# A branch hint at the top of every iteration of the expert loops and of the weight-tile loop

## What is computed

```
scores = softmax(xf @ gate_w.T);  topv, topi = top_k(scores, 2)
h  = relu(einsum('ecd,ehd->ech', de, fc1_w) + fc1_b)     # de: tokens sorted by expert
eo = einsum('ech,ehd->ecd', h, fc2_w) + fc2_b
out = x + sum(gathered eo * gates)
```

## Time and profile before

| | us |
|---|---|
| median of 3 runs | 1538.37 (1534.41 to 1542.68) |
| span of the profiled execution, first to last instruction | 1528.3 |
| TensorE matmuls busy | 1458.1 (95%) |
| VectorE busy | 820.2 (54%) |
| ScalarE busy | 537.3 (35%) |
| GpSimd busy | 285.5 (19%) |

### The profile page before, as it was taken

How to read it: one execution, slowest core, us unless ns; L and a number is a source line. 1 busy time by engine, 2 the same in 40 slices (tenths; PEclk the granted TensorE clock), 3 DMA queues, 4 the chain that set the end, 5 groups by cost and what they waited for, 6 DMA issues and landing times.

```text
span 1528.3 us, 21024 instructions
## 1 busy us (share of the span) xinstructions
PE 1458.1 (95%) x6470; PEld 1196.0 (78%) x6470; DVE 820.2 (54%) x1484; ACT 537.3 (35%) x871; POOL 285.5 (19%) x342
## 2 busy tenths in 40 slices
PE   7569999999999999999999999999999999999996
PEld 5348888788887888788887888788887888888885
DVE  6756634575355824566345753568245662558311
ACT  4234422343233422344233432344223432344221
POOL 1040030301204031120303121130312103030301
PEclk9669999999999999999999999999999999999998
DMA  8456431774319732394318742296324943196100
GB/s 291 179 138 146 100 102 36 160 146 106 75 41 180 151 97 55 96 175 98 110 28 160 159 103 65 53 190 134 91 55 107 174 90 103 34 181 137 56 0 27
DMA packets 446304, 169.30 MB, mean 111 GB/s; under 512 B 405248, under 2 KB 407433, under 8 KB 444274
## 3 DMA queue, kind: packets, MB, share of 16 engines
q1 hardware_dynamic: 293218, 84.01, 25.7%
q0 software_dynamic: 18096, 52.35, 12.1%
q10 hardware_dynamic: 134880, 31.47, 10.1%
HBM read 127.00 MB, written 41.03 MB: 110 GB/s over the span
## 4 chain that ended last, share of the span: by engine, by line
PE 95%; DVE 2%; issue 1%; DMA 0%; POOL 0%; ACT 0%; SPq 0%; DVEq 0%; POOLq 0%
PE hp L831 15%; PE hp L830 15%; PE eo L843 15%; PE eo L842 15%; PE eo L847 15%; PE hp L832 15%; PE hp L855 1%; PE eo L805 1%; PE hp L787 1%; PE hp L788 1%; DVE y_half L713 0%; DVE x_turned L713 0%; DMA rows<-in_x,gather_row 0%; PE xp L794 0%; DVE yT_lo L698 0%
## 5 line engine op out<-in xcount | busy, mean ns | idle before, releaser
L669 DVE TENSOR_TENSOR h_lo<-h_full,h_hi 128x512 fp32r<-128x512 f32 x256 | 176.6, 690 | 537.7 <-ACT h_full L451 537.6
L831 PE MATMUL hp<-yT_lo,w1T_hi 128*128 128x512 f32 x1020 | 397.7, 390 | 16.3 <-issue 16.3
L830 PE MATMUL hp<-yT_hi,w1T_hi 128*128 128x512 f32 x1020 | 398.1, 390 | 0.4 <-issue 0.2
L842 PE MATMUL eo<-w_hi,h_hi 128*128 128x512 f32 x1024 | 398.3, 389 | 0.0
L843 PE MATMUL eo<-w_lo,h_hi 128*128 128x512 f32 x1024 | 398.3, 389 | 0.0
L832 PE MATMUL hp<-yT_hi,w1T_lo 128*128 128x512 f32 x1020 | 397.5, 390 | 0.0
L448 ACT ACTIVATE h_hi<-hp,b_now 128x512 fp32r<-128x512 f32 x256 | 176.1, 688 | 617.7 <-PE hp L832 613.0
L847 PE MATMUL eo<-w_hi,h_lo 128*128 128x512 f32 x1024 | 273.7, 389 | 0.0
L832 PEld LDWEIGHTS hp<-yT_hi,w1T_lo 128*128 128x128 f32 x1020 | 192.0, 188 | 57.3 <-issue 17.6
L830 PEld LDWEIGHTS hp<-yT_hi,w1T_hi 128*128 128x128 f32 x1020 | 191.8, 188 | 42.1 <-issue 2.4
L842 PEld LDWEIGHTS eo<-w_hi,h_hi 128*128 128x128 f32 x1024 | 192.3, 188 | 40.0
(11 more groups left out here) (146 smaller groups left out, 717.0 us busy)
## 6 DMA issues: line engine op xcount, KB each, us to landing
w_raw<-in_L_ffn_fc_w SPq DMA_DIRECT2D x512, 64.0 KB
w_raw<-in_L_ffn_fc_w SPq DMA_DIRECT2D x128, 256.0 KB, 3.1
slots_dram<-x_blk ACTq DMA_DIRECT2D x30, 512.0 KB, 3.6
x_blk<-slots_dram ACTq DMA_DIRECT2D x240, 64.0 KB
out<-x_all SPq DMA_DIRECT2D x8, 1024.0 KB, 12.3
x_all<-in_x SPq DMA_DIRECT2D x7, 1024.0 KB, 13.9
b_bc<-in_L_ffn_fc_b POOLq DMA_DIRECT2D x8, 256.0 KB
x_all<-in_x SPq DMA_DIRECT2D x4, 256.0 KB, 4.1
```

What stands on the lines that cost most here:

```text
L669: dve.tensor_tensor(h_lo[:, c, :], h_full[:, :], h_hi[:, c, :].bitcast(F32), ALU.subtract).then_inc(h_ready, 1)
L830: pe.matmul(bank, w1T_hi[:, hh, q, :], yT_hi[:, par, q, :], start=(q == 0), stop=False)
L831: pe.matmul(bank, w1T_hi[:, hh, q, :], yT_lo[:, par, q, :], start=False, stop=False)
L842: pe.matmul(eo[:, b, :], h_hi[:, c, blk], w2_hi[:, hh, :], start=(hh == 0), stop=False)
```

## The change

The two loop heads are written with the general form of the same loop, for the same engine and the same range, with `hint_back_edge=True`. With it, each iteration begins with one more instruction on that engine, a branch prefetch hint, which names the compare-and-branch that closes the loop as likely taken. Nothing else is added or moved. The helper `experts` is used by four engines, so five loops get the hint. The last expert, written out, has none.

```diff
         def experts(eng, body):
 
-            with eng.Fori(0, E - 1) as e:
+            with nc.Fori(0, E - 1, engines=[eng.engine], hint_back_edge=True) as e:
                 body(e, False)
             body(E - 1, True)
...
-            with sp.Fori(1, E * HT // RAW) as m:
+            with nc.Fori(1, E * HT // RAW, engines=[sp.engine], hint_back_edge=True) as m:
                 for c in range(RAW):
                     sp.wait_ge(w1_T, RAW * m + (c - RAW + 1))
```

## The result

| | kernel before | changed kernel |
|---|---|---|
| median of the timed runs, us | 1536.39 (1531.74 to 1542.68, 4 runs) | 1510.38 (1509.55 to 1510.87, 4 runs) |
| span of the profiled execution, us | 1528.3 | 1507.9 |
| first to seventh closing branch of TensorE, us | 1065.0 | 1044.5 |

The ratio is 0.9834, with a 95% interval of 0.9801 to 0.9867: 26.0 us or 1.7% faster. Forecast were 1521 us and a range of 1515 to 1540. The direction and the place were right; the size was not, since the measured time lies 4.6 us under the range, and what the hint does there was not what the prediction took it to do.

The account below looks back on a forecast made before the run. TensorE was taken to set the time, losing 20.5 us at six loop back edges. The terms, -20.5 + 0.6 + 2.5 + 0.3 = -17.1 us, took 1538.4 to 1521.3, predicted 1521 us, range 1515 to 1540.

Parts of the forecast that it names:

- The base: Whole kernel: the median's 10.1 us above the profiled span stays unchanged, so the gain is subtracted from 1538.4 us.
- The 20.5 us at the edges: TensorE's six loop back edges: time lost beyond six whole bodies of 174.08 us, 20.5 us, counted as gain.
- The costs set against them: Remaining losses with the hint: 0.6 for TensorE's second fetch, 2.5 for VectorE, 0.3 for the last iteration.
- second fetch partly bare: Behind each TensorE back edge: the unhinted fetch of the next code block may start late; 0.1 us each, 0.6 in all.
- tile 2 late by VectorE: TensorE waits after each edge for a tile VectorE prepares, if VectorE's hint fails: 5.0 us, half taken, 2.5.
- last iteration falls through: Loop end: the hint says taken but the branch falls through, at worst one more TensorE fetch; 0.3 us taken.
- hint instructions: One more instruction per iteration on each hinted engine, including SyncE's 63: hidden, 0 us.
- What happens in one edge: TensorE's back edge: two code fetches in a row, the first hidden by the full queue, the second bare; 3.5 us lost.
- What the hint does: TensorE's back edge: the target's block comes in before the branch, so the second fetch moves under the full queue, 0.4 us spare.
- R1: TensorE's loop: the prefetched target may be thrown out before the branch, so all stays, 1538 us; chance 0.15.
- R2: TensorE's body: the armed hint displaces ordinary prefetch, so blocks are fetched on demand; slower, 1558 us; chance 0.10.
- R3: TensorE's edges: target prefetched but second fetch not covered, 1.5 to 2.5 us of 3.4 stay; 1527 to 1533; chance 0.10.

Follow-up runs that it names:

- the head at slot 200: Kernel before, no hint, with TensorE's loop head alone placed at instruction place 200 of a 256-instruction code block: 1515.05 us, ratio 0.989.
- TensorE at slot 0: Kernel before, no hint, with the loop heads of TensorE and VectorE placed at the first instruction of a code block: 1509.77 us, ratio 0.9855.
- the late hint at slot 239: Changed kernel with TensorE's hint some 33 instructions ahead of the branch and its loop head held 17 places ahead of a code block's end: 1522.54 us.
- the late hint: Changed kernel with TensorE's hint moved to some 33 instructions ahead of the closing branch, loop head not held in place: 1509.97 us, ratio 0.9856.

## Why the prediction was wrong in size

**The base: the step that failed most.** "The median of the runs lies 10.1 us above this span, which I take as unchanged." In the changed kernel the median lies 2.5 us above the profiled span. That is 7.6 of the 10.9 us by which 1521.3 missed; the other 3.3 are the costs below. Even with all costs at zero this base gave 1517.9. Outside the span there are only 1.6 to 2.1 us, in 29 later runs of the kernel before and the four of the changed one. So the rest of the 10.1 were longer spans of the other executions; and where a second and a third profile show such a span (1532.9 and 1535.9), the added time lies at the edges, most of it in the slower clock after more of the pauses. These are the pauses that the change removes, so this part of the spread goes with them: the changed kernel's four runs lie within 1.3 us, those of before within 11. Of the 26.0 us gained, 20.4 are the difference of the two profiled spans and 5.6 this base. Of the executions with the longest spans, 1537 to 1538.5, there is no profile, and the granted clock of the two longest is too high for the clock to be all of it; that their time lies at the edges too is not shown. Four runs are also few: two other kernels with TensorE's hint have a run some 4 us above their others.

**The 20.5 us at the edges** were right. From first to seventh branch are now 1044.5 us, the forecast's 1065.0 less 20.5. That they came out to the tenth doesn't speak for the mechanism: residence takes the whole pause away as well.

**The costs set against them**, 3.4 us in all, were zero:

| term | taken | measured |
|---|---|---|
| second fetch partly bare | 0.6 | 0: there is none; and where there is one (two experts per iteration), 0 |
| tile 2 late by VectorE | 2.5 | 0 with VectorE's hint; 2.4 without it, where 5.0 was the bound |
| last iteration falls through | 0.3 | 0: the branch takes 80 ns, TensorE shows no gap |
| hint instructions | 0 | 0: 31 to 39 ns in the median of an engine |

For VectorE I split the difference, since no row told how early a hint must come. With a body of its own that stays resident the question doesn't arise. One reading of the rows was off without a cost: 44 to 83 ns are branches of other engines and the one of TensorE that falls through; a taken branch of TensorE without a fetch takes 0.21 to 0.26 us, under the full queue.

**What happens in one edge**, two fetches of which the second is bare, is borne out by the head at slot 200. **What the hint does** was the step that had the wrong mechanism: it doesn't move the second fetch under the queue, it ends all fetches. I counted 9 packets per iteration, and used them against the Trainium skill's room of 2048 instructions; I didn't ask why a body that nearly fits is fetched again. It is one block that is too many, the one behind the loop, and it isn't part of it. By that the rivals were ranked on the wrong ground too. R1 feared that the head would be thrown out again between hint and branch; the fetch that would do that is the one that the hint suppresses.

**The Trainium skill's rule** that prefetch is purely sequential ("Runtime: NRT & Kernel Launch", "Instruction fetch mechanics") would have given 1538 here. The runs show otherwise: the measurement decides, and a hinted loop's head is fetched in place of the next block (two experts per iteration). That a taken branch whose target isn't there waits for a fetch holds, with 3.3 to 4.1 us on TensorE. But the section has that wait for each target outside a window of two pages, and TensorE at slot 0 goes back over its whole body of 1661 instructions without one.

**R2 and R3** did not occur. For the late hint at slot 239 something like R3 did: the head's block came partly ahead at four edges, and 10.4 us of edges were left.

No version beats the changed kernel by a measurable amount. In its profile TensorE has no gap over seven experts, so nothing is left to gain at these edges.

## What to carry to other kernels

TensorE's loop paid for instruction fetches when its body plus the one block fetched ahead behind its closing branch didn't fit together, and then for every block in every iteration. In another kernel look at the packets of the instruction queue per iteration and at the length of the taken branches of the engine that sets the time. A hint well ahead of the branch, or a loop head at the start of a block, turned a fetch of every block in each iteration into none here. One engine's loop may not be all of it: with TensorE freed, VectorE's fetches were late next. And before a change is sized from a single profile, ask whether that execution is a typical one of its kernel: if what the change removes is also what varies, the gain in the median is larger than the gain in the profile.

## What the runs showed of the hardware

- A fetch of code costs a taken branch of TensorE 3.3 to 4.1 us, and at the second edge the full matmul queue covered 3.9 of it. A queue that the first fetch has emptied covers little of the second: there four matmuls, 0.9 us.
- After a pause of 2.3 to 3.1 us TensorE's granted clock sometimes falls to the lower of its two levels for a while: after one of six such pauses in one execution, after four of six in two others. It fell after the pauses of 1.93 and 2.18 us of the late hint at slot 239 too. A mean of 0.83 over 10 us is about 1.7 us lost.
- A hint 2.8 us ahead of the branch, with the head held at slot 239, left branches of 2.4 us in the median and 4.07 at most; at the top of the body or in its middle it left 0.2.
- VectorE resumed 2.8 to 2.9 us after its branch with TensorE fetching nothing, 3.2 to 3.5 with it, so one engine's fetches seem to slow another's. No run separates the two otherwise.
- The hint on TensorE goes with 0.9 us more between the register move and the loop's first instruction, once, which I read as padding that moves the loop's head to the start of a block. The head's place wasn't read directly; the late hint, resident without a held head and not resident with one, speaks for it.
